# Grouped-query attention in a fused block: two score products in a row, then their two causal masks

## The chip, the cores and the metric

The kernel runs on one core of one Trainium2 chip. The metric is the device time of one execution in microseconds; of several runs the median is given. The core's engines run their own instruction queues side by side and meet at semaphores: PE (TensorE) multiplies matrices into PSUM banks, DVE (VectorE), ACT (ScalarE) and POOL (GpSimd) work elementwise, SP issues DMAs.

## The reference

The block has four stages on x of shape (2, 512, 256): a block-sparse causal convolution, a mixture-of-experts FFN, attention, and the FFN again. The change touches the attention alone:

```python
x = x + conv(_layernorm(x)); x = x + ffn(_layernorm(x)); x = x + attention(_layernorm(x)); x = x + ffn(_layernorm(x))
# attention: 16 heads, 4 key/value heads, head size 128, t = 512
q = _qknorm(x @ Wq.T, q_scale); k = _qknorm(x @ Wk.T, k_scale); v = x @ Wv.T
scores = jnp.einsum('bhtd,bhsd->bhts', q, k) * scale
scores = jnp.where(causal, scores, jnp.finfo(scores.dtype).min)
attn = jax.nn.softmax(scores, axis=-1)
out = jnp.einsum('bhts,bhsd->bhtd', attn, v)
return out.transpose(0, 2, 1, 3).reshape(b, t, N_HEADS * HEAD_DIM) @ Wo.T
```

## The kernel before

Every fp32 product is made of three fp32r matmuls, from operands split into a high and a low part (`triple`, the line L1360 of most matmuls): high by high, high by low, low by high.

The attention goes through four groups g, one for each key/value head. A group has NU = 8 units u, four heads for each of the two batches. The group is a software pipeline of steps k = 0 to 8 (`group_steps`). In step k PE makes the scores of unit k, the queries of unit k+1 (`query`), the values of unit k-2 (`values`) and the transposes of the probabilities of unit k-1 (`transposes`), then the sums of squares of the next queries (`query_sum`). Step 0 of the next group is joined to the end of a group together with a projection (`project`). Groups 0 to 2 run in a loop with register values, the last one is written out; in the loop step 7 and the end of a group also hold the products for the next group's keys and values. In step 0 of group 0 PE runs idle matmuls (`keep_busy`, L58) behind the queries.

The scores of a unit are four quarters j of 128 queries; quarter j sees the first 128(j+1) keys, so its triple writes 128 x 128(j+1) into PSUM (`S_BANK`: quarters 0 and 1 in bank 0, 2 in bank 1, 3 in bank 2). They run in the order 3, 2, 1, 0. Behind each triple one bf16 matmul of 128 columns (L1423: `ident_b` times `causal`) adds -1e30 above the diagonal of the quarter's last 128 columns and increments s_ready. So DVE can take the row maximum of quarter 3 (L1263) once s_ready has gone up by one, and that of quarter 2 once it has gone up by two. The order of all this is written out by hand; there is no scheduler.

DVE's queue in a step with scores: the low part of the transposed probabilities pt_lo, part 0 (L1247); the maxima of quarters 3 and 2; their bias (L1267), which also needs the query factor that POOL makes from qsum (L1166); pt_lo part 1; the maxima of quarters 1 and 0 and their bias; pt_lo part 2; the reciprocal of the row sums (L1293), which waits for ACT's four exponentials (L1097); four scalings of the probabilities (L1297); the low part of the next queries, qt_lo (L1217); the low part of the output, ot_lo (L1239); the query sum qsum, read from bank 1 (L1223). In steps 0 and 1 qt_lo comes before the reciprocal, and in step 0 of groups 1 to 3 a projection is added to X (L1254) after qsum.

PE waits for qt_lo_done ahead of the scores of a unit, for exp_done of the unit before ahead of each quarter, and, ahead of the first matmul of quarter 2, for qsum_done as well, since the query sums lie in the same PSUM bank as quarter 2.

Of the kernel before, what the change touches and what calls it, by code (L numbers as in the profile page):

```python
# [19 lines left out]
P = 128  # L20
# [25 lines left out]
NQ = C // P  # L46
# [8 lines left out]
def keep_busy(t, pm, bank, count):  # L55

    for _ in range(count):
        t.matmul(bank[:], pm["zeros"][:, 0:P], pm["zeros"][:], start=True, stop=True)  # L58
# [913 lines left out]
def attention_phase(nc, cm, pm, ps, ins, factors, prefetched, following, prefetch):  # L972

    with ExitStack() as ctx:
# [33 lines left out]
        S_BANK = ((0, 0), (0, P), (1, 0), (2, 0))  # L1008
# [9 lines left out]
        def steps_of(k):  # L1018


            return (k if k < NU else None, k - 1 if 1 <= k <= NU else None, k - 2 if 2 <= k <= NU else None,
                    k + 1 if k + 1 < NU else None)
# [330 lines left out]
        def _(t):  # L1353
            ln["tensor"](t, 0)

            def triple(dst, lhs, rhs, start, stop):

                (lh, ll), (rh, rl) = lhs, rhs
                for q, (l, r) in enumerate(((lh, rh), (ll, rh), (lh, rl))):
                    m = t.matmul(dst, l, r, start=start and q == 0, stop=stop and q == 2)  # L1360
                return m

            def keys_and_values(g, banks):
                for q in banks:
                    for j in range(2):
                        tok = slice((2 * q + j) * P, (2 * q + j + 1) * P)
                        for k in range(KH):
                            m = triple(ps[KV_BANK[q]][:, j * 2 * HD:(j + 1) * 2 * HD],
                                       (xt_hi[:, k, tok], xt_lo[:, k, tok]),
                                       (wkv_hi[:, k, :], wkv_lo[:, k, :]), k == 0, k == KH - 1)  # L1370
                    m.then_inc(s["kv_ready"], 1)

            def query(g, u):
                b, h = divmod(u, REP)
                if u >= 1:
                    t.wait_ge(s["qt_lo_done"], g * NU + u)
                tok = slice(b * C, (b + 1) * C)
                col = slice(h * HD, (h + 1) * HD)
                for k in range(KH):
                    m = triple(ps[Q_BANK][:], (wq_hi[:, k, col], wq_lo[:, k, col]),  # L1380
                               (xt_hi[:, k, tok], xt_lo[:, k, tok]), k == 0, k == KH - 1)
                m.then_inc(s["q_ready"], 1)
# [24 lines left out]
            def group_steps(g, ks, last, pending=False):  # L1407
                def scores(u):
                    b, sl = u // REP, u % 2
                    t.wait_ge(s["qt_lo_done"], g * NU + (u + 1))  # L1410
                    for j in reversed(range(NQ)):
                        bank, col = S_BANK[j]
                        if u >= 1 and j >= 1:

                            done = NQ * (u - 1) + (NQ if j == 1 else NQ - j)
                            t.wait_ge(s["exp_done"], g * NU * NQ + done)
                        if j == 2:
                            t.wait_ge(s["qsum_done"], g * NU + (u + 1))
                        q = slice(j * P, (j + 1) * P)
                        n = P * (j + 1)  # L1420
                        triple(ps[bank][:, col:col + n], (qt_hi[:, sl, q], qt_lo[:, sl, q]),
                               (kt_hi[:, b, 0:n], kt_lo[:, b, 0:n]), True, False)
                        t.matmul(ps[bank][:, col + n - P:col + n], pm["ident_b"][:], pm["causal"][:],  # L1423
                                 start=False, stop=True).then_inc(s["s_ready"], 1)

                def transposes(u):
                    sl = u % 2
                    t.wait_ge(s["prob_done"], g * NU * NQ + NQ * (u + 1))
                    for i in range(NQ):
                        bank = T_BANK + min(i, 2)  # L1430
                        if u >= 1 and i < 3:
                            t.wait_ge(s["pt_lo_done"], g * 3 * NU + (3 * (u - 1) + i + 1))
                        base = TOFF[i] - T_CUTS[min(i, 2)]
                        for j in range(i, NQ):
                            c = base + (j - i) * P
                            p0 = POFF[j] + i * P
                            m = t.transpose(ps[bank][:, c:c + P], prob[:, sl, p0:p0 + P], pm["ident"][:])
                        if i != 2:
                            m.then_inc(s["pt_ready"], 1)

                def values(u):
                    b, sl = u // REP, u % 2
                    if u >= 1:
                        t.wait_ge(s["ot_lo_done"], g * NU + u)
                    for i in range(NQ):
                        if i < 3:
                            t.wait_ge(s["pt_lo_done"], g * 3 * NU + (3 * u + i + 1))
                        src = slice(TOFF[i], TOFF[i + 1])
                        m = triple(ps[O_BANK][:, i * P:C], (v_hi[:, b * NQ + i, :], v_lo[:, b * NQ + i, :]),
                                   (pt_hi[:, sl, src], pt_lo[:, sl, src]), i == 0, i == NQ - 1)  # L1450
                    m.then_inc(s["o_ready"], 1)

                for k in ks:
                    score, turn, value, ahead = steps_of(k)
                    if score is not None:
                        scores(score)
                    if ahead is not None:
                        query(g, ahead)
                    if pending:
                        project(g - 1, 3)  # L1460
                    elif k == 0:
                        keep_busy(t, pm, ps[4], 8)
                    if k == NU - 1 and not last:
                        t.wait_ge(s["wkv_lo_done"], g + 2)
                        t.wait_ge(s["qt_lo_done"], g * NU + NU)
                        keys_and_values(g + 1, (0,))
                    if k == NU and last:
                        t.wait_ge(s["wo_lo_done"], g + 1)
                        t.wait_ge(s["qt_lo_done"], g * NU + NU)
                        project(g, 0, last, (0,))  # L1470
                    if k == 1:
                        t.wait_ge(s["acc_free"], g * 4 + 4)
                    if k == NU and not last:
                        t.wait_ge(s["exp_done"], g * NU * NQ + NU * NQ)
                        keys_and_values(g + 1, (1, 2))
                    if value is not None:
                        values(value)
                    if turn is not None:
                        transposes(turn)
                    if ahead is not None:  # L1480
                        query_sum(g, ahead)
                if NU in ks:
                    if not last:
                        keys_and_values(g + 1, (3,))
                    else:
                        project(g, 0, last, (1,))
                    values(NU - 1)
                    if last:
                        t.wait_ge(s["exp_done"], g * NU * NQ + NU * NQ)
                        project(g, 1, last)  # L1490

            def project(g, q, last=False, tiles=(0, 1)):

                b, j0 = divmod(2 * q, NQ)

                t.wait_ge(s["ot_lo_done"], g * NU + (REP * (b + 1)))
                for j in tiles:
                    tok = slice((j0 + j) * P, (j0 + j + 1) * P)
                    for h in range(REP):
                        m = triple(ps[Y_BANKS[last][q]][:, j * D:(j + 1) * D],  # L1500
                                   (ot_hi[:, b * REP + h, tok], ot_lo[:, b * REP + h, tok]),
                                   (wo_hi[:, h, :], wo_lo[:, h, :]), h == 0, h == REP - 1)
                if 1 in tiles:
                    m.then_inc(s["y_ready"], 1)
# [31 lines left out]
            t.wait_ge(s["kt_lo_done"], B)  # L1536
            query_sum(0, 0)
            group_steps(0, (0,), False)
            with t.Fori(0, NKV - 1) as g:
                group(g, False)  # L1540
# [95 lines left out]
```

## Time and profile before

| | us |
|---|---|
| median of 3 runs | 932.03 |
| lowest and highest run | 931.33, 932.53 |
| the profiled execution | 931.38 |
| span of its trace | 929.5 |

Busy in this execution: PE 902.2 us of the span, DVE 539.6, ACT 429.8, POOL 317.7. The scores run between 384 and 684 us from the span's start. Each row of a timeline gives the start and the duration in us; neighbouring instructions of one kind are merged, and x2 is their number. The end of a matmul is modelled, so for PE the distances between starts are what is to be read. A bracket at a row's end gives the idle time ahead of it and the engine and line that ended it.

### The profile page before, as it was taken

Reading aid. Unit: us, or ns where it says so; the run is one execution under the profiler, and the core shown is the slowest. Engines: PE = TensorE matmul, PEld = TensorE weight load, DVE = VectorE, ACT = ScalarE, POOL = GpSimd, SP = SyncE. Lnnn points to the kernel's source line nnn. Section 1 sums busy time; section 2 is a strip of 40 time slices with the busy share of each in tenths; the row PEclk is TensorE's granted clock in tenths of the full one; section 3 lists DMA queues with packets and bytes.
Section 4 is the critical chain, followed back from the end, with each engine's and each line's share of the span. In section 5 each row is a group of like instructions: output and inputs, shape, how many; then the busy total and the mean of one; then the engine's idle time right before and its main releaser. Section 6 shows DMA issues by size and latency. Waiting matters only on the chain. (4 is left out here: it accounts for less than half of the span.)

```text
span 929.5 us, 17066 instructions
## 1 busy us (share of the span) xinstructions
PE 902.2 (97%) x5753; PEld 785.0 (84%) x5753; DVE 539.6 (58%) x1360; ACT 429.8 (46%) x945; POOL 317.7 (34%) x286
## 2 busy tenths in 40 slices
PE   9999789999999998999999999999999999999998
PEld 7999656888888886778988997897886888888887
DVE  5999875433333337588678768867875533333333
ACT  4422335343433332576557647656653543433332
POOL 5111002355555564121121212112102256555563
PEclk9999899999999999999999999999999999999999
DMA  8899201111111102000100000000001111111111
GB/s 341 332 388 376 74 1 46 53 51 48 37 51 51 51 34 61 33 23 2 36 23 0 34 0 23 0 0 1 1 1 35 36 51 48 37 51 51 51 35 61
DMA packets 26096, 60.96 MB, mean 66 GB/s; under 512 B 3458, under 2 KB 11332, under 8 KB 26052
## 3 DMA queue, kind: packets, MB, share of 16 engines
q1 hardware_dynamic: 23748, 47.81, 15.6%
q0 software_dynamic: 2304, 12.58, 3.7%
q8 instruction: 26, 0.43, 0.2%
q14 instruction: 18, 0.15, 0.1%
HBM read 59.33 MB, written 1.05 MB: 65 GB/s over the span
## 5 line engine op out<-in xcount | busy, mean ns | idle before, releaser
L828 DVE TENSOR_TENSOR f_h<-f_scaled,bank 128x512 f32<-128x512 f32 (+1 forms) x90 | 60.8, 675 | 183.6 <-POOL f_scaled L729 183.6
L729 POOL TENSOR_TENSOR f_scaled<-f_act,f_gate_rows 128x512 f32<-128x512 f32 (+1 forms) x90 | 113.6, 1263 | 135.4 <-ACT f_act L660 135.0
L918 PE MATMUL bank<-f_xt_hi,f_w_lo 128*128 128x512 f32 (+1 forms) x400 | 157.1, 393 | 0.0
L918 PE MATMUL bank<-f_xt_hi,f_w_hi 128*128 128x512 f32 (+1 forms) x400 | 156.6, 392 | 0.0
L667 ACT ACTIVATE f_h_hi<-f_h 128x512 fp32r<-128x512 f32 (+2 forms) x102 | 63.6, 623 | 184.1 <-DVE f_h L828 184.1
L918 PE MATMUL bank<-f_xt_lo,f_w_hi 128*128 128x512 f32 (+1 forms) x400 | 123.6, 390 | 0.1
L1097 ACT ACTIVATE at_prob<-bank,at_sbias,at_qrs 128x512 f32<-128x512 f32 (+3 forms) x128 | 77.6, 617 | 85.5 <-DVE at_sbias L1267 85.5
L935 PE MATMUL bank<-f_w_lo,f_h_hi 128*128 128x256 f32 (+1 forms) x400 | 113.2, 283 | 0.0
L935 PE MATMUL bank<-f_w_hi,f_h_lo 128*128 128x256 f32 (+1 forms) x400 | 113.1, 283 | 0.0
L935 PE MATMUL bank<-f_w_hi,f_h_hi 128*128 128x256 f32 (+1 forms) x400 | 113.1, 283 | 0.0
L837 DVE TENSOR_TENSOR f_h_lo<-f_h,f_h_hi 128x512 fp32r<-128x512 f32 (+2 forms) x102 | 70.2, 688 | 73.1 <-ACT f_h_hi L667 73.0
L1166 POOL TENSOR_TENSOR at_qrs<-at_qsum,minus_half 128x4 f32<-128x4 f32 x32 | 32.8, 1024 | 208.4 <-DVE at_qsum L1223 208.4
L918 PEld LDWEIGHTS bank<-f_xt_lo,f_w_hi 128*128 128x128 f32 (+1 forms) x400 | 74.6, 187 | 17.2 <-DVE f_xt_lo L112 0.5
L660 ACT ACTIVATE f_act<-bank 128x512 f32<-128x512 f32 (+2 forms) x102 | 60.0, 590 | 58.7 <-PE bank L918 58.7
L918 PEld LDWEIGHTS bank<-f_xt_hi,f_w_hi 128*128 128x128 f32 (+1 forms) x400 | 75.1, 188 | 13.9 <-issue 0.9
L918 PEld LDWEIGHTS bank<-f_xt_hi,f_w_lo 128*128 128x128 f32 (+1 forms) x400 | 75.1, 188 | 13.0
L935 PEld LDWEIGHTS bank<-f_w_hi,f_h_hi 128*128 128x128 f32 (+1 forms) x400 | 76.4, 191 | 3.9
L935 PEld LDWEIGHTS bank<-f_w_hi,f_h_lo 128*128 128x128 f32 (+1 forms) x400 | 76.4, 191 | 3.6
L473 PEld LDWEIGHTS bank<-cv_onehot,cv_raw 128*128 128x128 f32 x640 | 74.8, 192 | 2.1 <-issue 0.5
L935 PEld LDWEIGHTS bank<-f_w_lo,f_h_hi 128*128 128x128 f32 (+1 forms) x400 | 76.4, 191 | 0.0
L716 POOL TENSOR_TENSOR f_w_lo<-f_wraw,f_w_hi 128x512 fp32r<-128x512 f32 x48 | 62.2, 1297 | 37.3 <-ACT f_w_hi L646 37.3
L473 PE MATMUL bank<-cv_onehot,cv_raw 128*128 128x64 f32 x640 | 74.5, 273 | 0.0
(186 smaller groups left out, 2004.6 us busy)
## 6 DMA issues: line engine op xcount, KB each, us to landing
cv_raw<-in_wconv SPq DMA_DIRECT2D x40, 512.0 KB, 6.9
cv_shared<-in_wtaps POOLq DMA_DIRECT2D x16, 768.0 KB, 7.5
f_wraw<-in_w SPq DMA_DIRECT2D x44, 256.0 KB, 2.7
f_wraw<-in_w SPq DMA_DIRECT2D x44, 128.0 KB, 2.5
at_wraw<-in_wqkv SPq DMA_DIRECT2D x3, 768.0 KB, 4.3
at_oraw<-in_wo SPq DMA_DIRECT2D x4, 512.0 KB, 3.6
X<-in_x_tiles SPq DMA_DIRECT2D x2, 512.0 KB, 7.9
f_wraw<-in_sw SPq DMA_DIRECT2D x4, 256.0 KB, 3.1
```

The costliest lines, as they stand in the source:

```text
L473: m = t.matmul(ps[q % BANKS][:].rearrange("p (w o) -> p w o", o=OB)[:, :, o], raw[c % RING][:, o * P:(o + 1) * P], onehot[:], start=True, ...
L660: a.activation(act[half][0:rows, cols], pg[half][0:rows, cols], ACT.Silu).then_inc(s["act_done"], 1)
L667: a.activation(h_hi[slot][0:rows, cols], h_f[half][0:rows, cols], ACT.Copy).then_inc(s["h_hi_done"], 1)
L716: g.tensor_tensor(w_lo[slot][:, 0:n], raw_views(m, slot, rows)[0], w_hi[slot][:, 0:n].bitcast(F32), ALU.subtract).then_inc(s["w13_lo_done" ...
L729: g.tensor_tensor(scaled[half][:, cols], act[half][:, cols], gate_rows[:, half * HALF + cols.start:half * HALF + cols.stop], ALU.mult).the ...
L828: v.tensor_tensor(h_f[half][0:rows, cols], src[half][0:rows, cols], pu[half][0:rows, cols], ALU.mult)\
L837: v.tensor_tensor(h_lo[slot][0:rows, cols], h_f[half][0:rows, cols], h_hi[slot][0:rows, cols].bitcast(F32), ALU.subtract).then_inc(s["h_lo ...
L918: mm = t.matmul(bank[half][0:rows, :], w, x, start=q == 0, stop=q == len(steps) - 1)
L935: mm = t.matmul(bank, h[hslot][0:rows, tok], w, start=first and q == 0 and j % 2 == 0, stop=last and q == 2, skip_group_check=True)
L1097: a.activation(prob[:, sl, POFF[j]:POFF[j + 1]], ps[bank][:, col:col + n], ACT.Exp, bias=sbias[:, sl, j:j + 1], scale=qrs[:, sl, j:j + 1], ...
L1166: p.tensor_tensor(qrs[:, u % 2, :], qsum[:, u % 2, :], pm["minus_half"][:, 0:NQ], ALU.pow)\
```

## The change

The body of the loop over quarters is split into two helpers, `products` and `mask`, which hold what stood there. Quarters 3 and 2 now run as products, products, mask, mask; quarters 1 and 0 run as before. The waits stay with the products. The order of the increments of s_ready, quarter 3 before quarter 2, is kept, and so is the work of DVE, ACT and POOL.

```diff
-                    for j in reversed(range(NQ)):
+
+                    def products(j):
                         bank, col = S_BANK[j]
                         if u >= 1 and j >= 1:
 
...
                         triple(ps[bank][:, col:col + n], (qt_hi[:, sl, q], qt_lo[:, sl, q]),
                                (kt_hi[:, b, 0:n], kt_lo[:, b, 0:n]), True, False)
-                        t.matmul(ps[bank][:, col + n - P:col + n], pm["ident_b"][:], pm["causal"][:],
+
+                    def mask(j):
+                        bank, col = S_BANK[j]
+                        t.matmul(ps[bank][:, col + P * j:col + P * (j + 1)], pm["ident_b"][:], pm["causal"][:],
                                  start=False, stop=True).then_inc(s["s_ready"], 1)
+
+                    products(3)
+                    products(2)
+                    mask(3)
+                    mask(2)
+                    for j in (1, 0):
+                        products(j)
+                        mask(j)
```

On PE, in the first step of the loop (step 1 of a group); at_s_ready goes up at each `causal` row, and what a row waits for stands in its bracket:

```order
 L1360 MATMUL bank<-at_kt_lo,at_qt_hi 128x512
-L1423 MATMUL bank<-causal,ident_b 128x128
-L1416 REGISTER_ALU
+L1417 REGISTER_ALU
 L1360 MATMUL bank<-at_kt_hi,at_qt_hi 128x384 [waits at_qsum_done,at_exp_done]
 L1360 MATMUL bank<-at_kt_hi,at_qt_lo 128x384
 L1360 MATMUL bank<-at_kt_lo,at_qt_hi 128x384
-L1423 MATMUL bank<-causal,ident_b 128x128
-L1416 REGISTER_ALU
+L1427 MATMUL bank<-causal,ident_b 128x128 x2
+L1417 REGISTER_ALU
 L1360 MATMUL bank<-at_kt_hi,at_qt_hi 128x256 [waits at_exp_done]
```

The mask of quarter 3 has moved behind the three 384-column products of quarter 2 and behind the wait for the query sum that stands ahead of them.

On DVE, in step 2 of a group, where the waits for these masks stand; these rows are the same in both programs:

```order
L1263 TENSOR_REDUCE at_smax<-bank 128x1 [waits at_s_ready]
L1262 REGISTER_ALU
L1263 TENSOR_REDUCE at_smax<-bank 128x1 [waits at_s_ready]
L1267 SCALAR_TENSOR_TENSOR at_sbias<-at_smax,at_qrs 128x2 [waits at_max_done,at_qrs_done]
L1244 REGISTER_ALU
```

Nothing moved here; the first of these rows is released by the mask of quarter 3, the second by that of quarter 2.

## Rows read from the trace of the kernel before

**Rows 1.** the page, its first part: busy microseconds, share of the span and instructions

```profile
PE 902.2 (97%) x5753; PEld 785.0 (84%) x5753; DVE 539.6 (58%) x1360; ACT 429.8 (46%) x945; POOL 317.7 (34%) x286
```

**Rows 2.** the waits of PE, 465:546: engine, line, releaser: total, times, longest

```profile
PE bank L1360 <- DVE at_pt_lo L1247: 1.2, 2, 0.7
PE bank L1360 <- DVE at_qt_lo L1217: 0.2, 1, 0.2
```

**Rows 3.** timeline of PE, 429.9:432.5: start, duration, engine, line, operation, operands

```profile
430.05 0.48 PE L1360 MATMUL bank<-at_kt_hi,at_qt_hi 128*128 128x512 f32 x1
...
430.84 0.23 PE L1423 MATMUL bank<-causal,ident_b 128*128 128x128 bf16 x1
430.88 0.42 PE L1360 MATMUL bank<-at_kt_hi,at_qt_hi 128*128 128x384 f32 x1
431.14 0.33 PE L1360 MATMUL bank<-at_kt_hi,at_qt_lo 128*128 128x384 f32 x1
431.31 0.34 PE L1360 MATMUL bank<-at_kt_lo,at_qt_hi 128*128 128x384 f32 x1
431.49 0.23 PE L1423 MATMUL bank<-causal,ident_b 128*128 128x128 bf16 x1
```

**Rows 4.** timeline of DVE, 430.1:437.9, the same step

```profile
431.11 1.20 DVE L1263 TENSOR_REDUCE at_smax<-bank 128x1 f32<-128x512 f32 x2
432.41 0.16 DVE L1267 SCALAR_TENSOR_TENSOR at_sbias<-at_smax,at_qrs 128x2 f32<-128x2 f32 x1
...
435.15 0.18 DVE L1293 RECIPROCAL at_rrec<-at_rsum 128x4 f32<-128x4 f32 x1 [0.77 <-ACT at_prob L1097]
...
436.56 0.68 DVE L1217 TENSOR_TENSOR at_qt_lo<-bank,at_qt_hi 128x512 fp32r<-128x512 f32 x1
```

**Rows 5.** timeline of PE, 437.2:438.3, where the next step begins

```profile
437.66 0.48 PE L1360 MATMUL bank<-at_kt_hi,at_qt_hi 128*128 128x512 f32 x1
```

**Rows 6.** timeline of DVE, 465:478.6, steps u = 0 and 1 of group 1

```profile
466.30 1.21 DVE L1263 TENSOR_REDUCE at_smax<-bank 128x1 f32<-128x512 f32 x2 [0.71 <-PE bank L1423]
...
472.94 0.16 DVE L1223 TENSOR_SCALAR at_qsum<-bank 128x4 f32<-128x4 f32 x1
...
473.84 1.18 DVE L1263 TENSOR_REDUCE at_smax<-bank 128x1 f32<-128x512 f32 x2
...
477.89 0.69 DVE L1217 TENSOR_TENSOR at_qt_lo<-bank,at_qt_hi 128x512 fp32r<-128x512 f32 x1 [1.66 <-ACT at_qt_hi L1070]
```

**Rows 7.** timeline of PE, 472.2:479.4, the starts of steps u = 1 and 2

```profile
472.76 0.48 PE L1360 MATMUL bank<-at_kt_hi,at_qt_hi 128*128 128x512 f32 x1
...
478.71 0.49 PE L1360 MATMUL bank<-at_kt_hi,at_qt_hi 128*128 128x512 f32 x1
```

**Rows 8.** timeline of DVE, 478.6:489.3, step u = 2 of group 1

```profile
480.88 1.15 DVE L1263 TENSOR_REDUCE at_smax<-bank 128x1 f32<-128x512 f32 x2
...
487.52 0.68 DVE L1217 TENSOR_TENSOR at_qt_lo<-bank,at_qt_hi 128x512 fp32r<-128x512 f32 x1
...
488.72 0.15 DVE L1223 TENSOR_SCALAR at_qsum<-bank 128x4 f32<-128x4 f32 x1
```

**Rows 9.** timeline of PE, 488:489, the start of step u = 3

```profile
488.33 0.49 PE L1360 MATMUL bank<-at_kt_hi,at_qt_hi 128*128 128x512 f32 x1 [0.16 <-DVE at_qt_lo L1217]
```

**Rows 10.** timeline of PE, 391:392, step u = 1 of group 0

```profile
391.13 0.48 PE L1360 MATMUL bank<-at_kt_hi,at_qt_hi 128*128 128x512 f32 x1
```

**Rows 11.** timeline of DVE, 392.5:394, the same step

```profile
392.78 1.15 DVE L1263 TENSOR_REDUCE at_smax<-bank 128x1 f32<-128x512 f32 x2
```

**Rows 12.** timeline of DVE, 679.5:689.9, last group, step u = 7 and after

```profile
679.88 0.68 DVE L1217 TENSOR_TENSOR at_qt_lo<-bank,at_qt_hi 128x512 fp32r<-128x512 f32 x1
...
688.08 1.61 DVE L1247 TENSOR_TENSOR at_pt_lo<-bank,at_pt_hi 128x512 fp32r<-128x512 f32 x3
```

**Rows 13.** timeline of PE, 680.9:689, the same stretch

```profile
680.97 0.48 PE L1360 MATMUL bank<-at_kt_hi,at_qt_hi 128*128 128x512 f32 x1
...
688.90 0.47 PE L1360 MATMUL bank<-at_pt_hi,at_v_hi 128*128 128x512 f32 x1 [0.17 <-DVE at_pt_lo L1247]
```

## The prediction

> **What bounds the kernel now.** I read the page first, then the waits of PE in one attention group, then the timeline of PE, DVE and ACT step by step. PE is busy 97% of the span [rows 1]. In group 1 of the attention it waits for another engine 1.4 us in all [rows 2], so nearly everywhere PE's own queue sets the pace. But a busy engine may still be one that is only just served in time, so the second question is how late the other engines are. In a usual step PE starts the scores at 430.05 and the next ones at 437.66, a period of 7.61 us [rows 3, 5]. The next scores need qt_lo of the next head. DVE writes it at the end of a chain that hangs on the first mask of this step: mask of quarter 3 at 430.84, row maxima at 431.11, bias at 432.41, then four exponentials on ACT, the reciprocal at 435.15 (DVE had stood 0.77 us for ACT), the four scalings, qt_lo at 436.56 to 437.24 [rows 3, 4]. PE takes it up at 437.66: 0.42 us to spare. How long PE needs between the end of qt_lo and its start, where it does wait, is shown by step 3 of group 1: qt_lo ends at 487.52 + 0.68 = 488.20, PE starts at 488.33, so 0.13 us [rows 8, 9]. The real slack is 0.42 - 0.13 = 0.29 us. The last of these places, in the last group, reads the same: 679.88 + 0.68 = 680.56 against 680.97, 0.41 us [rows 12, 13]. There are 16 such places, the starts of steps 4 to 7 in each of 4 groups; in three of them the gap is smaller, in none larger than 0.44 us.
>
> **Part 1, the masks in a row.** Mask 3 starts at 430.84, the first product of quarter 2 0.04 us later, but the second product comes after 0.26 us where the following ones come every 0.175 us (431.14, 431.31, 431.49) [rows 3]. A mask between products thus costs PE 0.04 + 0.085 = 0.125 us: its own pass, and the weights of the product behind it, which so short a matmul doesn't cover. After the change the products of quarter 2 stand behind a 512-column product and lose nothing; the second mask stands behind the first and should cost its own pass, 0.04 to 0.06 us. Two masks cost 0.125 + 0.055 = 0.18 instead of 0.25 us. The gain is 0.07 us for each of 32 score steps, 2.2 us if PE set the pace in all of them; bounds are 0 (the second mask pays as much as the first) and 0.085. The Trainium skill (TensorE: Matmul & The Clock Gate, Back-to-back issue gap) gives about 81 ns for each 128-column matmul in a stream with weight loads; by it, as an estimate, the gain would be 0.125 - 0.081 = 0.044 us a step, 1.4 us in all, and no row here shows two masks in a row.
>
> **Part 2, mask 3 comes later.** It is now issued behind the three products of quarter 2: 3 x 0.175 = 0.525 us after its old place. Does DVE feel all of it? In group 1, step 0, DVE stood idle 0.71 us until that mask and started its maxima at 466.30 [rows 6], and in the usual step it starts 0.27 us after the mask [rows 3, 4], so yes. It gets a little back: the pair of maxima takes 1.20 us where the second waits for mask 2, and 1.15 us where both masks had long been done (step 2) [rows 4, 8]. After the change both are done together, so the bias and all behind it (exponentials, reciprocal, scalings, qt_lo) come 0.525 - 0.05 = 0.475 us later, counted from the start of the scores. Bounds: 0.40 and 0.55.
>
> *Usual steps.* qt_lo would end 437.24 - 430.05 + 0.475 = 7.665 us after the scores began, and PE resumes 0.13 later: 7.795 instead of 7.61, that is 0.185 us more. PE's own gain of 0.07 is lost there, since it only lengthens the wait. Sixteen such places: 16 x 0.185 = 2.96 us.
>
> *Step 2 of each group.* DVE takes the maxima at 480.88, 2.17 us after the scores began at 478.71, because it is still busy with step 1 [rows 7, 8]. A mask at 0.79 + 0.525 = 1.315 after the start is still early enough. This step moves as a block, 0.
>
> *Steps 0 and 1 of groups 1 to 3 (the steps behind a project).* Step 0 delays the scalings by 0.475. Behind them DVE reads the query sum, at 472.94 until 473.10 [rows 6]; it would end at 473.575. Here a wait has changed sides: the first product of quarter 2 waits for qsum_done, and mask 3 used to stand ahead of that wait and now stands behind it. PE would be there at 472.76 - 0.07 + 0.79 = 473.48; with 0.13 us to release it starts at 473.70, its weight load uncovered (0.09, as behind any wait, by the difference between 0.26 and 0.175 above), so mask 3 comes at 473.70 + 0.09 + 0.525 = 474.32 and the maxima at 474.59 instead of 473.84: 0.75 late [rows 6, 7]. The pair took 1.18 and will take 1.15: 0.72 us. From there the chain is unbroken before and after: DVE waits 1.66 us for ACT, writes qt_lo from 477.89 to 478.58 and PE starts at 478.71, 0.13 behind [rows 6, 7]. So 3 x 0.72 = 2.16 us, the gain of PE in step 0 being inside it. In group 0 the maxima of step 1 start 392.78 - 391.13 = 1.65 us after the scores [rows 10, 11], later than the new mask would allow (1.315 + 0.27 = 1.585), and what precedes is padded with idle matmuls; I take 0, at most +0.4.
>
> *The ends of the groups.* In groups 0 to 2 the new keys and values cover DVE; PE sets the pace and gains 0.07 each: -0.21 us. In the last group there is no such cover: PE stands 0.17 us for pt_lo at 688.90, and DVE writes that behind the scalings of step 7 [rows 12, 13]. It moves by the whole 0.475: +0.48 us.
>
> **Sum.** 2.96 + 0 + 2.16 - 0.21 + 0.48 = 5.4 us. The profiled execution took 931.38 us, its span is 929.5 us, and the median of the runs is 932.03, 0.65 above it. The change adds to span and time alike: 936.8 for that execution, 937.4 on the median, 0.6% slower. What a measurement of this kernel can tell from no change is about 0.2%, 1.9 us.
>
> **Rivals.**
> (a) *PE sets the pace throughout, and the change gains.* If the lateness of qt_lo stays under the slack less PE's gain, 0.29 - 0.07 = 0.22 us, PE never waits and the 0.07 us come out 32 times: 932.03 - 2.2 = 929.8. It takes a DVE that recovers more than 0.3 of the 0.525 us. For it speaks PE at 97% [rows 1]; against it that DVE is idle at both ends of the stretch (0.71 before the maxima, 0.77 before the reciprocal), so nothing in it can be shortened. The Trainium skill (Perfetto Trace Analysis, Identifying the Most-Contended Engine) would have one optimize the engine with the highest occupancy first and warns that matmul busy is a bad measure; read plainly it points to this rival. I give it 0.08.
> (b) *Only the places with a wait already in the rows get later.* The usual steps absorb the shift, the opening steps and the tail don't: 2.2 - 0.2 + 0.5 = 2.5 us, less the gain of 16 usual steps (1.1): 1.4 us, 933.4, within what can be told. It would need a lateness between 0.22 and 0.29 us. 0.07.
> (c) *The wait for the query sum bites in every usual step.* Once PE is released by qt_lo, DVE has still to write ot_lo and then the sum; in step 3 that sum ends at 488.72 + 0.15 = 488.87, 0.54 us after the scores began [rows 8, 9], and 0.67 with the release, where the products of quarter 2 are due at 0.79 but their weights should start loading with the product before, at 0.55. If the load is uncovered by 0.09 us each time, the 16 places and 3 more give 19 x 0.09 = 1.7 us on top: 939.1. 0.17.
> (d) The order isn't changed as it says: the instructions of the new program show the new order in every step, 0.
>
> **The numbers.** The forecast, 0.6 of the chance, is 937.4, with bounds of its own: lateness 0.40 gives 16 x 0.11 + 3 x 0.65 - 0.2 + 0.4 = 3.9 (935.9), 0.55 with +0.4 in group 0 gives 16 x 0.26 + 3 x 0.8 - 0.2 + 0.55 + 0.4 = 7.3 (939.3). A release of 0.05 instead of 0.13 would take another 1.3 off. The range reaches from 934.6 to 940.0 and takes in (c); about 0.15 lies below, with (a) and (b). The rest, 0.08, is for a case I haven't seen, mostly above. Faster by over 0.2%: 0.08; within: 0.08; slower: 0.84.
>
> **What would show it.** In the new trace: mask 3 at 1.31 us after the scores' start and mask 2 some 0.05 behind; the maxima at 1.58 instead of 1.06; PE waits for qt_lo at sixteen more places, a period of 7.80 instead of 7.61; a wait for qsum in step 1 of groups 1 to 3, with the period of step 0 to 1 a little shorter and of step 1 near 6.7 instead of 5.95; step 2 unchanged at 9.6; the end of a group in the loop 0.07 shorter. Wrong would be: no new wait for qt_lo (then (a) or (b)), a mask pair that costs 0.25 us, or products of quarter 2 that start later than 0.8 in usual steps (then (c)). A drop of the granted clock by the short new idle times would make it worse than all of these.

## The result and the profile after

| | before | after |
|---|---|---|
| median, us | 932.10 (4 runs) | 937.52 (4 runs) |
| lowest and highest run | 931.33, 932.53 | 937.13, 937.95 |
| the profiled execution | 931.38 | 937.33 |
| span of its trace | 929.5 | 935.5 |
| start of the first scores in it | 384.76 | 385.88 |
| from there to the end | 544.77 | 549.64 |

The changed kernel is slower: ratio 1.0059, 95% interval 1.0045 to 1.0073. The spans differ by 6.0 us, but 1.1 us of that lies ahead of the first scores, where the two programs are the same. Over the ten profiled kernels of this document, which have the same program up to there, the first scores started between 384.8 and 386.4 us. So what the change does is read from the first scores on: 549.64 - 544.77 = 4.9 us. Behind the attention's last product all ten take 225.8 us, so the variation lies ahead. TensorE's granted clock was 1.00 through the attention in both traces; the clock has no part in the difference.

The first line of the page looks like the one of before [rows 1]; one would not see from it that anything happened.

```profile
PE 905.3 (97%) x5753; PEld 788.6 (84%) x5753; DVE 536.6 (57%) x1360; ACT 429.5 (46%) x945; POOL 317.7 (34%) x286
```

The waits of PE over group 1 (465 to 549 us; engine, line, releaser, total, times, longest), which answer to [rows 2]:

```profile
PE bank L1360 <- DVE at_pt_lo L1247: 1.2, 2, 0.7
PE bank L1360 <- DVE at_qt_lo L1217: 0.3, 2, 0.2
```

These rows don't show the loss either. PE stands at qt_lo twice by this view, for 0.3 us, although every usual step became longer. The modelled ends of the matmuls ahead of the wait reach over it. The distances between starts tell more. The timeline of PE in a usual step, against [rows 3, 5]:

```profile
431.76 0.49 PE L1360 MATMUL bank<-at_kt_hi,at_qt_hi 128*128 128x512 f32 x1
...
432.56 0.33 PE L1360 MATMUL bank<-at_kt_hi,at_qt_hi 128*128 128x384 f32 x1
432.73 0.34 PE L1360 MATMUL bank<-at_kt_hi,at_qt_lo 128*128 128x384 f32 x1
...
433.08 0.29 PE L1427 MATMUL bank<-causal,ident_b 128*128 128x128 bf16 x2
...
439.57 0.49 PE L1360 MATMUL bank<-at_kt_hi,at_qt_hi 128*128 128x512 f32 x1
```

The first product of quarter 2 starts 0.80 us after the scores' start and the second 0.17 behind it, so what the mask between them had cost is gone. Mask 3 starts at 1.32 us (the row with x2 is both masks; their two records start 0.067 us apart). The next scores start at 439.57: the period is 7.81 us where it was 7.61. The timeline of DVE over the same step, against [rows 4]:

```profile
430.95 0.68 DVE L1217 TENSOR_TENSOR at_qt_lo<-bank,at_qt_hi 128x512 fp32r<-128x512 f32 x1
...
433.35 1.16 DVE L1263 TENSOR_REDUCE at_smax<-bank 128x1 f32<-128x512 f32 x2 [0.45 <-PE bank L1427]
...
438.76 0.69 DVE L1217 TENSOR_TENSOR at_qt_lo<-bank,at_qt_hi 128x512 fp32r<-128x512 f32 x1
```

The maxima start at 433.35, 1.59 us after the scores, and now with 0.45 us of idle time ahead that PE's mask ends. The chain behind them is as long as it was, but for 0.04 us: the pair of maxima takes 1.16 us instead of 1.20. qt_lo ends at 438.76 + 0.69 = 439.45, and PE starts at 439.57, 0.12 to 0.13 behind. Before, 0.42 us lay between the two.

From the starts of the scores, the steps of one group in both traces (us; group 1 stands for the loop's groups, the last column is the end of a group with its keys, values and projections):

| step of group 1 | 0 | 1 | 2 | 3 | 4 | 5 | 6 | 7 and end |
|---|---|---|---|---|---|---|---|---|
| before | 7.51 | 5.95 | 9.62 | 7.64 | 7.61 | 7.61 | 7.61 | 27.59 |
| after | 7.38 | 6.58 | 9.62 | 7.81 | 7.81 | 7.81 | 7.81 | 27.54 |

A usual step is one of steps 3 to 6 of a group, which end with the start of the scores of steps 4 to 7. Summed over the four groups: 16 usual steps +3.00 us, steps 0 and 1 +1.52 (nothing in group 0, about 0.5 in each other group), step 2 nothing, the three group ends in the loop -0.17, the tail of the last group +0.5. That is 4.9 us.

### The profile page after: what moved, and what is told of

Its sections match the earlier page's. It is cut to its first block and busy times, and to the rows that moved or that the text cites. A ratio compares the mean times of both kernels' runs of the same rounds, so it can differ in the third digit from the quotient of the medians.

```text
span 935.5 us, 17066 instructions
## 1 busy us (share of the span) xinstructions
PE 905.3 (97%) x5753; PEld 788.6 (84%) x5753; DVE 536.6 (57%) x1360; ACT 429.5 (46%) x945; POOL 317.7 (34%) x286
```

## Experiments

Each kernel below was run beside the kernel before on the same chip; the stretch is the time from the first scores to the end of its trace (544.77 before, 549.64 after the change), which leaves out the variation ahead of the attention. Beside the first four kernels the one before had a median of 932.46 us (20 runs), beside the last four 932.28 (27 runs).

| kernel | median, us | ratio to before, 95% interval | stretch | usual step | steps 0, 1 of group 1 |
|---|---|---|---|---|---|
| late_only | 940.27 | 1.0084, 1.0067 to 1.0101 | 552.36 | 7.94 | 7.51, 6.56 |
| mask3_after1 | 932.75 | 1.0006, 0.9996 to 1.0015 | 545.39 | 7.63 | 7.48, 6.04 |
| mask3_after2 | 933.67 | 1.0013, 1.0003 to 1.0023 | 546.23 | 7.64 | 7.44, 6.21 |
| old_in_u1 | 936.06 | 1.0040, 1.0026 to 1.0054 | 548.48 | 7.81 | 7.38, 6.29 |
| qtlo_early | 936.46 | 1.0044, 1.0028 to 1.0059 | 549.02 | 7.78 | 7.38, 6.58 |
| qtlo_qsum_early | 932.23 | 0.9998, 0.9988 to 1.0007 | 544.53 | 7.56 | 7.38, 6.57 |
| before_relief | 931.49 | 0.9991, 0.9982 to 1.0000 | 543.81 | 7.61 | 7.51, 5.96 |
| pair_where_free | 930.25 | 0.9980, 0.9971 to 0.9989 | 542.91 | 7.56 | 7.51, 5.96 |

### late_only: the lateness without PE's new order

To the kernel before, in DVE's `maxima`:

```diff
-                    v.wait_ge(s["s_ready"], g * NU * NQ + (NQ * u + (NQ if j < 2 else NQ - j)))
+                    v.wait_ge(s["s_ready"], g * NU * NQ + (NQ * u + (NQ if j < 2 else 2)))
```

> PE's order is that of the kernel before; only DVE waits for both masks ahead of the maximum of quarter 3. Theory (the loss is the lateness of the maxima, handed on to qt_lo): mask 2 stands at 1.435 us after the scores' start against 0.79 for mask 3, so all behind it is 0.645 - 0.05 = 0.60 late; usual steps 7.19 + 0.60 + 0.13 = 7.92 us instead of 7.61; steps 0 and 1 of groups 1 to 3 together 0.7 longer, tail 0.6; about 7.7 us in all, 939.7. Rival (the loss is in PE's new order, the masks in a row or the wait for the query sum ahead of mask 3): usual steps stay at 7.61, time 932 to 933.

PE's timeline in a usual step, and then DVE's:

```profile
431.97 0.49 PE L1360 MATMUL bank<-at_kt_hi,at_qt_hi 128*128 128x512 f32 x1
...
432.77 0.23 PE L1423 MATMUL bank<-causal,ident_b 128*128 128x128 bf16 x1
...
433.42 0.23 PE L1423 MATMUL bank<-causal,ident_b 128*128 128x128 bf16 x1
...
439.90 0.49 PE L1360 MATMUL bank<-at_kt_hi,at_qt_hi 128*128 128x512 f32 x1
```

```profile
433.69 1.16 DVE L1263 TENSOR_REDUCE at_smax<-bank 128x1 f32<-128x512 f32 x2 [0.58 <-PE bank L1423]
...
439.08 0.68 DVE L1217 TENSOR_TENSOR at_qt_lo<-bank,at_qt_hi 128x512 fp32r<-128x512 f32 x1
```

PE runs its masks where it always did, at 0.80 and 1.45 us, and DVE begins 0.27 behind the second. The period is 439.90 - 431.97 = 7.93 us. With no change on PE at all, the kernel is slower than the changed one, since its maxima are 0.13 us later still and it has no gain from the masks. So the lateness is enough to make the loss. The stretch grew by 7.6 us, 7.7 were expected; group 0's first steps lost 0.2 us of it, which nothing had been put down for, and the other terms came out a little smaller.

### mask3_after1 and mask3_after2: how late may the mask be

To the changed kernel: the three matmuls of quarter 2 are written out, with mask 3 behind the first or behind the second of them.

```diff
-                    products(2)
-                    mask(3)
+                    products(2, between=2)
                     mask(2)
```

(`between=1` in the other; `products` calls mask(3) ahead of the matmul with that number, counted from 0.)

> Mask 3 is put behind the first of the three products of quarter 2, mask 2 stays behind the last. Theory: mask 3 at 0.79 + 0.175 = 0.965, everything behind it 0.125 late, under the slack of 0.29 us, so usual steps stay at 7.61 with PE setting the pace; 0.1 in steps 0 and 1 of groups 1 to 3 and 0.125 in the tail: 932.5. Rival (every delay of the mask costs in proportion, a quarter to a third of the loss of 4.9 us): usual steps 7.67, 933.5 or more.

> Mask 3 is put behind the second of the three products of quarter 2. Theory: mask 3 at 1.14, everything behind it 0.30 late, 7.19 + 0.30 + 0.13 = 7.62 us a usual step, just at the slack, so the loss is still nearly nothing there; steps 0 and 1 of groups 1 to 3 0.27 longer each pair, tail 0.3: 933.3. Rival (in proportion): usual steps 7.74, 935.3.

In these two kernels L1427 is the line of the products and L1431 that of the masks. PE, then DVE, in a usual step of mask3_after2:

```profile
430.37 0.49 PE L1427 MATMUL bank<-at_kt_hi,at_qt_hi 128*128 128x512 f32 x1
...
431.52 0.23 PE L1431 MATMUL bank<-causal,ident_b 128*128 128x128 bf16 x1
...
438.00 0.49 PE L1427 MATMUL bank<-at_kt_hi,at_qt_hi 128*128 128x512 f32 x1
```

```profile
431.79 1.16 DVE L1263 TENSOR_REDUCE at_smax<-bank 128x1 f32<-128x512 f32 x2 [0.28 <-PE bank L1431]
...
437.19 0.68 DVE L1217 TENSOR_TENSOR at_qt_lo<-bank,at_qt_hi 128x512 fp32r<-128x512 f32 x1
```

Here the mask stands at 1.15 us and the maxima at 1.42. qt_lo ends at 437.19 + 0.68 = 437.87, and PE starts at 438.00, 0.13 behind it, which is just the release; the period is 7.63. The same step of mask3_after1, PE and then DVE:

```profile
430.63 0.48 PE L1427 MATMUL bank<-at_kt_hi,at_qt_hi 128*128 128x512 f32 x1
...
431.59 0.23 PE L1431 MATMUL bank<-causal,ident_b 128*128 128x128 bf16 x1
...
438.26 0.48 PE L1427 MATMUL bank<-at_kt_hi,at_qt_hi 128*128 128x512 f32 x1
```

```profile
437.26 0.68 DVE L1217 TENSOR_TENSOR at_qt_lo<-bank,at_qt_hi 128x512 fp32r<-128x512 f32 x1
```

Here the mask stands at 0.96, the maxima at 1.22, qt_lo ends 0.32 us ahead of the next scores, and the period is 7.63 too. Moving the mask from 0.96 to 1.15 thus cost this step nothing, and moving it on to 1.32 costs 0.18. Over all 16 usual steps the two kernels lose 0.3 and 0.5 us, the changed one 3.0; over the stretch 0.6, 1.5 and 4.9. So the loss has an edge where the slack ends, and no proportion. The steps behind a projection have no slack before the change (PE starts 0.13 us behind qt_lo there) and no edge: 5.95 grows to 6.04, 6.21 and 6.58 as the mask moves.

Step 4 of the loop's groups is an exception in mask3_after2 (7.68 to 7.69). Its first bias (L1267) takes 0.20 to 0.22 us instead of 0.16, and in the kernel before 0.32. POOL's and DVE's rows of that step in group 0, kernel before:

```profile
416.23 1.28 POOL L1147 TENSOR_TENSOR at_wkv_lo<-at_wraw,at_wkv_hi 128x512 fp32r<-128x512 f32 x1
417.20 0.32 DVE L1267 SCALAR_TENSOR_TENSOR at_sbias<-at_smax,at_qrs 128x2 f32<-128x2 f32 x1
```

The bias ends with POOL's instruction, at 417.52 against 417.51. The ten traces hold 49 rows of this bias that are longer than 0.17 us, and each ends 0.01 to 0.02 us behind the POOL instruction beside it; why, no run here shows. This is also why the slack before the start of step 5 was the smaller one in these three groups. After the change the maxima are so late that POOL is done when the bias comes, and it takes 0.16 us.

### old_in_u1: the wait that changed sides

To the changed kernel:

```diff
-                    products(3)
-                    products(2)
-                    mask(3)
-                    mask(2)
+                    if u == 1:
+                        for j in (3, 2):
+                            products(j)
+                            mask(j)
+                    else:
+                        products(3)
+                        products(2)
+                        mask(3)
+                        mask(2)
```

> The changed kernel, but unit 1 of each group keeps the old order, mask 3 directly behind its products and ahead of the wait for the query sum. Theory: in step 1 of groups 1 to 3 the maxima start when DVE has added the projection, 1.42 us after the scores' start instead of 1.76, in group 0 about 1.3 instead of 1.59; step 1 is 0.3 shorter in each group, 1.2 us in all, and usual steps stay at 7.81: 936.3. Rival (step 1 is long because step 0 delays DVE, not because of the wait ahead of the mask): step 1 stays at 6.57, 937.5.

First the changed kernel in step 1 of group 1, PE and then DVE, against [rows 6, 7]:

```profile
474.49 0.47 PE L1360 MATMUL bank<-at_kt_hi,at_qt_hi 128*128 128x512 f32 x1
...
475.38 0.41 PE L1360 MATMUL bank<-at_kt_hi,at_qt_hi 128*128 128x384 f32 x1
...
475.98 0.29 PE L1427 MATMUL bank<-causal,ident_b 128*128 128x128 bf16 x2
```

```profile
474.68 0.48 DVE L1297 TENSOR_SCALAR at_prob<-at_prob,at_rrec 128x512 f32<-128x512 f32 x1
475.07 0.15 DVE L1223 TENSOR_SCALAR at_qsum<-bank 128x4 f32<-128x4 f32 x1
...
476.25 1.16 DVE L1263 TENSOR_REDUCE at_smax<-bank 128x1 f32<-128x512 f32 x2 [0.42 <-PE bank L1427]
```

The query sum ends at 475.22, and the first product of quarter 2 starts 0.16 behind it, at 0.89 us instead of 0.80. Both masks stand behind that, at 1.49, and DVE is idle 0.42 us. Now old_in_u1 in the same place:

```profile
473.99 0.47 PE L1360 MATMUL bank<-at_kt_hi,at_qt_hi 128*128 128x512 f32 x1
...
474.78 0.23 PE L1427 MATMUL bank<-causal,ident_b 128*128 128x128 bf16 x1
474.88 0.41 PE L1360 MATMUL bank<-at_kt_hi,at_qt_hi 128*128 128x384 f32 x1
```

```profile
474.65 0.68 DVE L1254 TENSOR_TENSOR X<-X,bank 128x512 f32<-128x512 f32 x1
475.48 1.16 DVE L1263 TENSOR_REDUCE at_smax<-bank 128x1 f32<-128x512 f32 x2
```

Mask 3 is back at 0.79. The product behind it waits for the query sum here too (0.10 us after the mask instead of 0.04), but no one waits for that product yet. DVE starts its maxima at 1.49, 0.15 us behind the addition to X. Step 1 is 6.29 instead of 6.58, 0.3 us in each of these groups (0.46 in the last). What is left above 5.95 is the delay that step 0 hands over. In group 0 nothing changed beyond 0.02, where 0.3 had been expected: DVE goes into these maxima without a pause, at 1.58 us in place of 1.59, held by its own work. The stretch is 1.2 us shorter, as expected, but that is partly luck: 1.0 us comes from step 1 of three groups, where four had been counted, and the rest from small differences elsewhere.

### qtlo_early: one deadline removed

To the changed kernel, on DVE:

```diff
                         for j in range(NQ):
+                            if j == NQ - 1 and ahead is not None and k > 1:
+                                query_low(g, ahead)
                             pj = prob[:, sl, POFF[j]:POFF[j + 1]]
...
-                    if ahead is not None and k > 1:
-                        query_low(g, ahead)
                     if value is not None:
                         output_low(g, value)
```

> The changed kernel, with qt_lo written by DVE between the third and the fourth scaling instead of behind all four (steps 2 to 6), so the scores get their input 0.4 us earlier. Theory: qt_lo is no longer the bound, but the query sum becomes it. DVE reaches it no earlier than before, 6.77 us after its maxima; PE releases the products of quarter 2 0.13 later, and the maxima follow them 0.88 behind: a usual step of 7.78, hardly less than 7.81. About 937.2 against 937.5. Rival (qt_lo is the only obstacle): PE sets the pace, 7.54 a step, 933.2.

PE, then DVE, in a usual step:

```profile
431.43 0.48 PE L1360 MATMUL bank<-at_kt_hi,at_qt_hi 128*128 128x512 f32 x1
...
432.36 0.41 PE L1360 MATMUL bank<-at_kt_hi,at_qt_hi 128*128 128x384 f32 x1
...
432.96 0.29 PE L1427 MATMUL bank<-causal,ident_b 128*128 128x128 bf16 x2
...
439.21 0.48 PE L1360 MATMUL bank<-at_kt_hi,at_qt_hi 128*128 128x512 f32 x1
```

```profile
430.47 0.68 DVE L1217 TENSOR_TENSOR at_qt_lo<-bank,at_qt_hi 128x512 fp32r<-128x512 f32 x1
...
432.07 0.15 DVE L1223 TENSOR_SCALAR at_qsum<-bank 128x4 f32<-128x4 f32 x1
...
433.23 1.16 DVE L1263 TENSOR_REDUCE at_smax<-bank 128x1 f32<-128x512 f32 x2 [0.41 <-PE bank L1427]
```

qt_lo ends at 431.15, 0.28 us ahead of the scores, so that deadline is met. But the query sum ends at 432.22, 0.79 us into the scores, and the first product of quarter 2 starts only at 432.36, 0.93 us in; the masks stand at 1.53 and DVE is idle 0.41 us. The period is 7.78, the bound that had been worked out. The next wait stood only 0.03 us below the one that was removed. The kernel is 0.6 us better in the stretch than the changed one, and the usual steps gave only 0.2 of that. Step 2 fell from 9.62 to 9.32 in all four groups, twice what PE's row of waits there would allow (0.16 us [rows 9]), while each end of a group in the loop grew by 0.2 (27.76 instead of 27.54).

### qtlo_qsum_early: both deadlines removed

As qtlo_early, and:

```diff
-                    if value is not None:
-                        output_low(g, value)
                     if ahead is not None and not early_sum:
                         query_sum(g, ahead)
+                    if value is not None:
+                        output_low(g, value)
```

> As qtlo_early, and DVE reads the query sum ahead of ot_lo instead of behind it. Theory: the sum ends 0.34 to 0.4 us after the scores' start, both deadlines are met, PE sets the pace with its two masks in a row: usual steps 7.54, step 2 about 9.5 instead of 9.62; the extra in step 1 of groups 1 to 3 and in the tail stays. 4.3 + 0.5 us less than the changed kernel: 932.7. Rival (the masks' lateness costs by another path too, such as pt_lo or ACT's queue): usual steps stay over 7.7.

```profile
430.89 0.48 PE L1360 MATMUL bank<-at_kt_hi,at_qt_hi 128*128 128x512 f32 x1
...
431.67 0.34 PE L1360 MATMUL bank<-at_kt_hi,at_qt_hi 128*128 128x384 f32 x1
...
432.21 0.29 PE L1427 MATMUL bank<-causal,ident_b 128*128 128x128 bf16 x2
...
438.45 0.48 PE L1360 MATMUL bank<-at_kt_hi,at_qt_hi 128*128 128x512 f32 x1
```

```profile
431.07 0.16 DVE L1223 TENSOR_SCALAR at_qsum<-bank 128x4 f32<-128x4 f32 x1
...
432.48 1.16 DVE L1263 TENSOR_REDUCE at_smax<-bank 128x1 f32<-128x512 f32 x2
```

Of PE (above) and DVE (below): the sum ends 0.34 us into the scores, the products of quarter 2 start at 0.78, mask 3 at 1.32. The maxima start at 1.59, exactly as late as in the changed kernel, and the period is 7.56. So the late mask costs a usual step nothing once the two results that PE needs no longer stand at the end of DVE's chain. The stretch is 5.1 us shorter than the changed kernel's, 4.8 had been expected, again with step 2 as the difference. Against the kernel before, the time is the same. That comparison flatters the pair of masks, since step 2 gained from DVE's new order and not from the masks; the fair one follows below.

### before_relief and pair_where_free: a kernel that uses it

before_relief is the kernel before with the same two moves on DVE. pair_where_free has them too, and the pair of masks only where it is covered:

```diff
+                    if 2 <= u and not (last and u == NU - 1):
+                        products(3)
+                        products(2)
+                        mask(3)
+                        mask(2)
+                    else:
+                        for j in (3, 2):
+                            products(j)
+                            mask(j)
```

> The kernel before with the same new order on DVE (qt_lo ahead of the last scaling, the query sum ahead of ot_lo). Theory: usual steps are PE's, 7.61 as before; only step 2, where PE stood for qt_lo, gets 0.13 shorter: 0.5 us less than before, not to be told from no change. If DVE's new order were good by itself, usual steps would get shorter too.

> DVE's new order, and the two masks in a row only for units 2 to 7 (in the last group 2 to 6); units 0 and 1, and 7 of the last group, keep the old order. Theory: usual steps 7.54, step 2 about 9.5, steps 0 and 1 and the tail as in the kernel before, the loop's group ends 0.05 shorter: 16 x 0.07 + 4 x 0.13 + 3 x 0.05 = 1.8 us less than before, ratio 0.998. Rival (the gain of the masks is given back elsewhere): ratio 1.000.

The distances between starts in before_relief are 7.61 for all usual steps but 9.32 for step 2, 1.0 us in the stretch, and the ratio's interval ends at 1.0000. Step 2 gives 1.2 us in the four groups, and the tail of the last group takes 0.3 back, which had not been expected: PE starts the product that waits for pt_lo 8.27 us after the last scores instead of 7.93. DVE's new order by itself thus does nothing for usual steps. With that order on both sides, the pair of masks in every step (qtlo_qsum_early) still loses 544.53 - 543.81 = 0.7 us: PE's gain in the usual steps, 0.7 us, is less than the 1.5 us that steps 0 and 1 lose. pair_where_free has 7.55 to 7.57 in usual steps, 9.32 to 9.34 in step 2, and 7.51 and 5.96 in steps 0 and 1 as before. It is faster than the kernel before, ratio 0.9980 with 0.9971 to 0.9989. Of its 1.9 us in the stretch about half is DVE's order and half the masks: before_relief has 543.81 us, pair_where_free 542.91, 0.9 less (16 x 0.05 + 3 x 0.05 = 0.95). Run beside each other, 11 times each, their medians are 931.49 and 930.25.

A pair of masks for quarters 1 and 0 as well, whose maxima wait for all four masks anyway, should cost no lateness. It wasn't tried: both quarters lie in one PSUM bank, the accumulation of one would be open while the other starts, and no run here shows whether that is safe.

## Why the prediction was right

937.4 was forecast and 937.52 measured, and the mechanism was the forecast one: the late mask reaches PE again through qt_lo. One term of the sum was clearly mis-sized, steps 0 and 1. Point by point:

- **What bounds the kernel.** The slack was read as 0.29 us behind the release of 0.13. mask3_after1 and mask3_after2 found its end where it had been put: at most 0.04 us a step at a lateness of 0.30 (but for the three steps 4, with 0.07 to 0.08), 0.20 at 0.475.
- **The masks in a row.** Estimated at 0.07 us a step, 0.055 for the second mask. The two masks start 0.067 us apart, and the first product of quarter 1 follows 0.03 behind the second. Where PE sets the pace the step went from 7.61 to 7.56 (before_relief against qtlo_qsum_early), so 0.05: the products behind the pair start 0.06 us earlier than before, and 0.01 of it is gone at the end of the step. The Trainium skill (TensorE: Matmul & The Clock Gate, Back-to-back issue gap) gives 81 ns for a matmul of 128 columns in a stream with weight loads; the second mask here stood 67 ns behind the first, though it loads its weights too.
- **The lateness.** Mask 3 was forecast at 1.31 and stands at 1.32, the maxima at 1.58 and 1.59. The pair of maxima took 1.16 us instead of 1.20, so the 0.05 given back were 0.04.
- **Usual steps.** 7.80 forecast, 7.81 measured in the loop and 7.77 in the last group; 2.96 us against 3.00. In the last group PE starts 0.05 us behind qt_lo instead of 0.13, as the forecast had allowed for in a side remark. The rival in which the query sum bites in every such step didn't happen in the loop: the products of quarter 2 start at 0.80 and follow each other after 0.17 us. In the last group a trace of it shows: there the sum ends 0.61 us into the scores instead of 0.54, the second product of quarter 2 follows after 0.21 us, and mask 3 stands at 1.36. qtlo_early shows how near it was in the loop.
- **Step 2.** Forecast unchanged, and it is (9.62). The reason given, that DVE takes its maxima only 2.17 us after the scores began, is what the trace after the change shows too. There is a second one that the forecast didn't see: the first bias of this step takes 1.41 us and ends with POOL's at_wo_lo (L1174), so that in this step the chain hangs on POOL and not on the masks.
- **Rival (b).** Its price and its condition don't fit: between 0.22 and 0.29 us of lateness the usual steps would keep only part of the 1.1 us that it takes off.
- **Steps 0 and 1 of groups 1 to 3.** This term was mis-sized: 3 x 0.72 = 2.16 us forecast, 1.52 measured. Two things were missed, and the first can be read from ACT. Before the change, in step 0, ACT goes from the read of the second sum to the squares of the queries like this:

```profile
469.14 0.20 ACT L1097 ACTIVATION_READ_ACCUMULATOR at_prob<-bank,at_sbias,at_qrs 128x1 f32 x1
469.30 0.60 ACT L1069 ACTIVATE at_qsq<-bank 128x512 f32<-128x512 f32 x1
```

and after it, like this:

```profile
471.48 0.20 ACT L1097 ACTIVATION_READ_ACCUMULATOR at_prob<-bank,at_sbias,at_qrs 128x1 f32 x1
471.57 0.59 ACT L1069 ACTIVATE at_qsq<-bank 128x512 f32<-128x512 f32 x1
```

The distance is 0.16 us before and 0.09 after: ACT had been waiting some 0.07 us for PE's queries, and this wait took up part of the lateness. The second is the query sum of step 1. The forecast let it move with the scalings ahead of it. Before the change the last of them stood here, and the sum at 472.94 [rows 6]:

```profile
472.41 0.48 DVE L1297 TENSOR_SCALAR at_prob<-at_prob,at_rrec 128x512 f32<-128x512 f32 x1
```

That is 0.05 us between the end of one and the start of the other, where the rows of step 1 above have the sum start 0.09 us before the recorded end of the last scaling (475.07 against 474.68 + 0.48). So before, DVE had been waiting some 0.14 us for PE's sums, and that took up another part. Counted from the scores of step 0, the sum's end moved from 7.85 to 8.11 us, 0.26, where the forecast had 0.475: 0.07 and 0.14 of it had gone into waits that the forecast had not looked for. The step of the forecast that fell short is thus the one that handed the lateness of step 0 on undiminished to the query sum. Step 0 also became 0.13 us shorter for PE, not 0.07. What did that beyond the mask's 0.067 I can't say; the difference builds up over the matmuls between the masks and the end of the step.
- **Ends of the groups and tail.** -0.21 forecast, -0.17 measured. The tail was +0.48 against +0.5. DVE, then PE, against [rows 12, 13]:

```profile
694.08 1.61 DVE L1247 TENSOR_TENSOR at_pt_lo<-bank,at_pt_hi 128x512 fp32r<-128x512 f32 x3
```

```profile
694.91 0.47 PE L1360 MATMUL bank<-at_pt_hi,at_v_hi 128*128 128x512 f32 x1 [0.17 <-DVE at_pt_lo L1247]
```

PE still stands 0.17 us for pt_lo, at 8.46 us after the last scores instead of 7.93.

The sum of the terms was 5.4 us, the trace has 4.9 behind the first scores. That the medians differ by 5.4 is thus in part luck: the stretch ahead of the attention differed by up to 1.6 us between the ten profiled executions, and the interval of the ratio, 4.2 to 6.8 us, holds both.

The Trainium skill (Perfetto Trace Analysis, Identifying the Most-Contended Engine) would have the most-contended engine optimized first, and judges TensorE by its use of the peak FLOPs and by the busy share of the weight loads, not by that of the matmuls. PE is the busiest engine by either share here, with 84% and 97%. Taking time off PE did pay where nothing became late by it, 0.9 us in pair_where_free against before_relief; but this change took time off PE too, and the kernel got slower. The busy share doesn't show that.

## What to carry to other kernels

An instruction that signals is worth more than its own duration: before moving it behind other work, follow what it releases until it comes back to the engine it stands on, and compare the delay with the slack there, less the time from a result's end to its use. Look also for waits that it is moved past, since these now hold the signal too. And where one deadline on an engine is relieved, the next result in that engine's queue may be due almost as soon; here it took two moves on DVE, the first of them nearly worthless alone for the usual steps, to take their loss away. To judge such a repair, give it to the kernel before as well: 0.7 us of the loss was left, in steps that the moves don't reach, and only the kernel that pairs the masks just where nothing waits for them gained.

## What the runs showed of the hardware

- A bf16 matmul of 128 columns that follows another with the same weights starts 0.067 us behind it, though its weights are loaded again. One alone between fp32r products takes 0.12 to 0.13 us of PE's time, two in a row 0.18.
- From the end of DVE's result to the start of a matmul that waits for it 0.13 us pass in the loop and 0.05 us in the group written out behind it, where it waits for qt_lo.
- The view of waits gave 0.3 us for PE at qt_lo over a group in which four steps had each grown by 0.2 us. For PE the distances between starts showed what the idle times didn't.
- A small VectorE instruction (128x2, L1267) that started beside a TENSOR_TENSOR of POOL ended 0.01 to 0.02 us behind it in all 49 cases, after 0.20 to 1.41 us instead of 0.16.
